# Four edits to a fused adapter/FFN/Sinkhorn kernel: low parts of the stacked operand formed once, root table loaded elsewhere, Sinkhorn shares 11, 12, 13, 13, base-weight blocks split sooner (and three smaller ones)

## The reference, cut to what matters

```python
# x: (8, 256, 1024); layer 0: a weight per sample, then a quantised FFN
h = einsum('bij,bkj->bik', x, weight[ids_cond])            # A: conditioned product
h = layernorm(h) * gamma + beta
h = fake_quant(h) @ fake_quant(w1).T + b1
x = x + (fake_quant(gelu(h)) @ fake_quant(w3).T + b3)
# layer 1: base linear + LoRA of rank 16, then stream mixing
base  = einsum('bsi,oi->bso', x, weight) + bias
y     = base + scale[id] * (x @ A[id].T @ B[id].T)
n     = y * rsqrt(mean(y*y) + eps)
H_res = sinkhorn(n @ W_res.T + base_res, 50 iterations)     # 4 x 4 per token
H_pre, H_post = softmax(n @ W_pre.T + ...), softmax(n @ W_post.T + ...)
H_res = (1 - g) * I + g * H_res
out   = x + H_res-mix(y) + (H_pre-gather(y) @ W_branch) spread by H_post
```

## Time and profile before

| | |
|---|---|
| median of 3 runs | 791.6 us (790.79 to 793.91) |
| profiled execution: its own time | 791.53 us |
| its span | 789.7 us |
| busy: TensorE, VectorE, ScalarE, GpSimd | 727.0, 555.2, 374.2, 68.0 us |
| mean granted TensorE clock | 0.971 of full |

### The profile page before, as it was taken

One profiled execution on the slowest core, in us unless ns is written; L12 is line 12 of the kernel. 1 busy time (PEld: TensorE's weight loads), 2 busy tenths in 40 slices (PEclk: granted clock), 3 DMA queues, 4 the chain that ended last, 5 costly groups with the idle time before them and its releaser, 6 DMA issues.

```text
span 789.7 us, 10179 instructions
## 1 busy us (share of the span) xinstructions
PE 727.0 (92%) x3228; PEld 490.2 (62%) x3228; DVE 555.2 (70%) x1933; ACT 374.2 (47%) x682; POOL 68.0 (9%) x40
## 2 busy tenths in 40 slices
PE   9989999999999999989998999998999994799937
PEld 6555444364656666434765788887878773567626
DVE  4558675537888887782865513517898988999985
ACT  2253735316556454543543643436324342699614
POOL 0002000200202022533031000000000000000000
PEclk9999999999999999999999999999999998799969
DMA  7959974243555542826032203113032157665406
GB/s 297 411 171 405 268 271 150 81 161 98 187 182 187 187 173 81 310 76 227 27 134 92 99 26 120 55 67 118 5 120 71 52 170 251 216 216 184 138 0 213
DMA packets 54279, 124.32 MB, mean 157 GB/s; under 512 B 8015, under 2 KB 33743, under 8 KB 48722
## 3 DMA queue, kind: packets, MB, share of 16 engines
q1 hardware_dynamic: 52930, 120.94, 44.1%
q10 hardware_dynamic: 1296, 2.74, 0.9%
HBM read 98.47 MB, written 25.19 MB: 157 GB/s over the span
## 4 chain that ended last, share of the span: by engine, by line
PE 52%; DVE 20%; ACT 10%; DMA 10%; issue 5%; SPq 2%; POOL 1%; ACTq 0%; DVEq 0%
PE PS L1080 15%; PE PS L969 10%; PE PS L905 8%; DMA stage<-w_dram 4%; PE PS L894 4%; DMA wscale_scratch<-wsc 3%; PE PS L958 2%; PE PS L1232 2%; PE PS L1192 2%; PE PS L1002 2%; DVE xp L1494 2%; DMA out_dram<-mr 2%; ACT blk L834 2%; DVE hbuf L1293 2%; PE PS L1186 2%
## 5 line engine op out<-in xcount | busy, mean ns | idle before, releaser
L905 PE MATMUL PS<-w_raw,x_raw 128*128 128x512 f32 x336 | 150.0, 600 | 4.7 <-DMA x_raw<-x_tr_dram 3.4
L905 PEld LDWEIGHTS PS<-w_raw,x_raw 128*128 128x128 f32 x336 | 63.1, 193 | 76.8 <-issue 73.2
L1080 PE MATMUL PS<-w_hi,xT_hi 128*128 128x512 f32 x256 | 103.3, 404 | 0.0
L1080 PE MATMUL PS<-w_hi,xT_lo 128*128 128x512 f32 x256 | 100.5, 393 | 0.0
L1080 PE MATMUL PS<-w_lo,xT_hi 128*128 128x512 f32 x256 | 100.3, 392 | 0.0
L514 POOL TENSOR_TENSOR xres<-xres,vecs 128x1024 f32<-128x1024 f32 x16 | 42.8, 2696 | 311.5 <-DMA xres<-x_tok_dram 311.5
L1399 DVE TENSOR_TENSOR xT_lo<-PS,xT_hi 128x512 fp32r<-128x512 f32 x32 | 20.6, 682 | 66.0 <-ACT xT_hi L662 65.8
L1588 DVE TENSOR_REDUCE ksum<-kprod 128x16 f32<-128x64 f32 x392 | 66.1, 209 | 0.0
L595 ACT ACTIVATE qT<-PS,round_c 128x512 bf16<-128x512 f32 x64 | 40.1, 678 | 45.7 <-PE PS L958 45.6
L969 PE MATMUL PS<-w3q,qT 128*128 128x512 bf16 x256 | 58.0, 379 | 1.0 <-ACT qT L595 1.0
L969 PE MATMUL PS<-w1q,qT 128*128 128x512 bf16 x256 | 57.9, 379 | 0.8 <-ACT qT L595 0.7
(11 more groups left out here) (190 smaller groups left out, 1393.8 us busy)
## 6 DMA issues: line engine op xcount, KB each, us to landing
w_raw<-cond_w_dram SPq DMA_DIRECT2D x31, 1024.0 KB, 5.7
x_raw<-x_tr_dram SPq DMA_DIRECT2D x32, 256.0 KB, 6.4
stage<-w_dram SPq DMA_DIRECT2D x16, 512.0 KB, 12.1
xres<-x_tok_dram SPq DMA_DIRECT2D x8, 1024.0 KB, 8.3
x_scratch<-x1buf SPq DMA_DIRECT2D x16, 512.0 KB, 5.1
x1n<-x_scratch SPq DMA_DIRECT2D x16, 512.0 KB, 6.1
y_scratch<-y SPq DMA_DIRECT2D x16, 512.0 KB, 3.1
stage<-base_w_nat_dram SPq DMA_DIRECT2D x8, 512.0 KB, 12.5
```

The source lines that it names most:

```text
L905: mm = pe.matmul(PS[:, 2 * t + h, :], x_raw[pr][:, c, t * P:(t + 1) * P], w_raw[pr][:, c, h * H2:(h + 1) * H2], start=(pr == 0 and c == 0) ...
L1080: pe.matmul(PS[:, 2 * t + h, :], xx[:, c, t * P:(t + 1) * P], ws[c // 2][:, c % 2, h * H2:(h + 1) * H2], start=(c == 0 and xx is xT_hi and ...
```

## The change

1. A DRAM table `low_dram` (129 rows) receives the low parts of all eight samples' rows and of the bias row. `load_rows` (SP) loads 8 x 16 rows and their scales after the stage loads of sample 1; ScalarE writes `all_hi` and `one_hi`, VectorE the differences, in place; `store_rows` stores them. Head columns follow at samples 4 to 6 (`store_heads`, `load_heads`, `store_head_rows`). In layer 1, rows 32 to 48 of `estage` are loaded from `low_dram`; the VectorE instruction of `lo_stacks` is gone, and `low_rank` waits for `e_hi`.
2. In `step_b` a Sqrt of a constant stands ahead of `evac_y(b, 1)`.
3. `B_ITERS` is (11, 12, 13, 13), with shares 2,3,3,3; 3,3,3,3; 3,3,3,4; 3,3,3,4, and none behind sample 7.
4. `split_hi(2)` stands in sample 6, `split_hi(3)` sooner in sample 7, `split_lo(2)` ahead of an `add_b3`. The heads' store and its wait leave the queue's place ahead of the loads `load_x1n`.
5. `keep_warm`: 48 transposes of the identity on TensorE, three iterations before the second Sinkhorn's end. The last tile's add and store are done in two halves.

```diff
@@ sync @@
+            def load_rows():
+                for b in range(NB):
+                    a = sp.value_load(ids[0:1, 1, bass.ds(b, 1)], min_val=0, max_val=NA - 1)
+                    r = slice(b * RANK, (b + 1) * RANK)
+                    sp.dma_start(all_in[r, :], lora_bt[bass.ds(a, 1), :, :].rearrange("a r n -> (a r) n")).then_inc(all_ld, 16)
+                    sp.dma_start(all_scale[r, :], scaling[bass.ds(a, 1), :].to_broadcast([RANK, 1])).then_inc(all_ld, 16)
...
             load_stage(KC + 7)
+            sp.wait_ge(st_T, 2 * (KC + 4))
+            sp.dma_start(one_in[:, :], bias_row).then_inc(all_ld, 16)
+            load_rows()
             load_xres(0)
             load_w(2, 0)
...
             for s in range(2, NB - 1):
+                if s == 2:
+                    store_rows()
+                if s == 4:
+                    store_heads()
+                if s == 5:
+                    load_heads()
+                if s == 6:
+                    store_head_rows()
...
-            sp.wait_ge(c_sb, 2)
-            sp.dma_start(c_dram.rearrange("a r n -> (a r) n"), csb[:, 0, :]).then_inc(c_st, 16)
-            sp.dma_start(cb_dram, csb[0:1, 1, :]).then_inc(c_st, 16)
-            sp.wait_ge(c_st, 32)
...
-                wait(sp, e_lo, b)
-                for r in (0, 32, 64):
+                wait(sp, e_hi, b)
+                sp.dma_start(estage[32:32 + RANK, :], low_dram[RANK * b:RANK * (b + 1), :]).then_inc(e_ld, 16)
+                for r in (0, 64):
@@ gpsimd @@
             split_lo(0)
             split_lo(1)
+            split_lo(2)
             add_b3(GUEST - 2)
-            split_lo(2)
             split_lo(3)
@@ scalar @@
             evac_stage(KC + 4)
+            act.wait_ge(all_ld, 16 * (2 * NB + 1))
+            nc.scalar.activation(all_hi[:, :], all_in[:, :], ACT.Copy, scale=all_scale[:, 0:1]).then_inc(all_high, 1)
+            nc.scalar.activation(one_hi[:, :], one_in[:, :], ACT.Copy).then_inc(all_high, 1)
             evac_T(0, 1, 1)
             gelu(0, 0)
...
                     evac_xT(b + 1, 0)
+                nc.scalar.activation(hd[:, 6, 0:1], round_c[:, 0:1], ACT.Sqrt)
                 evac_y(b, 1)
@@ tensor @@
             def low_rank(b, t, h):
                 pe.wait_ge(ls_done, b + 1)
-                pe.wait_ge(e_lo, b + 1)
+                pe.wait_ge(e_hi, b + 1)
...
+            def keep_warm():
+                pe.wait_ge(hs_step, 2)
+                pe.wait_ge(k_step[0], K0 + 3 + K_OPS * (SINKHORN - 1 - WARM_ITERS))
+                for i in range(WARM_LAST):
+                    pe.transpose(PS[:, SEL_BANK + i // 4 % 2, (i % 4) * P:(i % 4 + 1) * P], ident[:, :], ident[:, :])
...
+            keep_warm()
             select(1)
@@ vector @@
             quantise_stage(KC + 6)
             dve.wait_ge(bias_ld, 16 * 2)
             dve.wait_ge(swld, 16)
+            dve.wait_ge(all_high, 2)
+            nc.vector.scalar_tensor_tensor(out=all_in[:, :], in0=all_in[:, :], scalar=all_scale[:, 0:1],
+                                           in1=all_hi[:, :], op0=ALU.mult, op1=ALU.subtract).then_inc(all_low, 1)
+            nc.vector.tensor_tensor(one_in[:, :], one_in[:, :], one_hi[:, :], ALU.subtract).then_inc(all_low, 1)
             finish_w1(0, 0)
...
             def lo_stacks(b):
-                dve.wait_ge(e_hi, b + 1)
-                nc.vector.scalar_tensor_tensor(out=es[32:64, :], in0=estage[32:64, :], scalar=e_scale[32:64, 0:1],
-                                               in1=es[32:64, :], op0=ALU.mult, op1=ALU.subtract).then_inc(e_lo, 1)
                 dve.wait_ge(f_done, b + 1)
...
-                        n = B_ITERS // 4
-                        iterations(0, (b - NB // 2) * B_ITERS + i * n, n)
+                        k = b - NB // 2
+                        lo, hi = B_ITERS[k] * i // 4, B_ITERS[k] * (i + 1) // 4
+                        iterations(0, sum(B_ITERS[:k]) + lo, hi - lo)
```

More of the change, by code:

```diff
@@ L70, in adaln_ffn @@
         part_s.close()
+        part_e = ctx.enter_context(ExitStack())
+        for i in range(2 * PAIRS):
+            sb_in(part_e, f"below_rows{i}", [P, D], F32)
+        all_in = sb_in(part_e, "all_in", [NB * RANK, D], F32)
+        all_hi = sb_in(part_e, "all_hi", [NB * RANK, D], F32R)
+        one_in = sb_in(part_e, "one_in", [1, D], F32)
+        one_hi = sb_in(part_e, "one_hi", [1, D], F32R)
+        part_e.close()
+        part_n = ctx.enter_context(ExitStack())
+        heads_in = sb_in(part_n, "heads_in", [NB * RANK, NH], F32)
+        heads_hi = sb_in(part_n, "heads_hi", [NB * RANK, NH], F32R)
+        bias_in = sb_in(part_n, "bias_in", [1, NH], F32)
+        bias_hi = sb_in(part_n, "bias_hi", [1, NH], F32R)
+        part_n.close()
         part_w = ctx.enter_context(ExitStack())
@@ L206, in adaln_ffn @@
         vec_ld, bias_ld, ids_ld, ones_set = sem("vec_ld"), sem("bias_ld"), sem("ids_ld"), sem("ones_set")
-        high = [sem(f"high{i}") for i in range(PAIRS)]
-        low = [sem(f"low{i}") for i in range(PAIRS)]
+        high = [sem(f"high{i}") for i in range(PAIRS - 1)]
+        low = [sem(f"low{i}") for i in range(PAIRS - 1)]
         id_zero, id_set = sem("id_zero"), sem("id_set")
@@ L258, in adaln_ffn @@
         SK_OPS = 12
-        B_ITERS = 12
+        B_ITERS = (11, 12, 13, 13)
+        K0 = 3 + K_OPS * (SINKHORN - 1) + 1
+        WARM_ITERS, WARM_LAST = 3, 48
         @block.sync
@@ L311, in load_scales, with store_rows, load_heads, store_head_rows @@
                              ).then_inc(swld, 16)
+            def load_rows():
[4 more added lines that the diff above has]
+                    sp.dma_start(all_scale[r, :], scaling[bass.ds(a, 1), :].to_broadcast([RANK, 1])).then_inc(all_ld, 16)
+            def store_rows():
+                sp.wait_ge(all_low, 2)
+                sp.dma_start(low_dram[0:NB * RANK, 0:D], all_in[:, :]).then_inc(all_st, 16)
+                sp.dma_start(low_dram[NB * RANK:NB * RANK + 1, 0:D], one_in[:, :]).then_inc(all_st, 16)
+            def load_heads():
+                sp.wait_ge(c_st, 32)
+                sp.dma_start(bias_in[:, :], cb_dram).then_inc(all_ld, 16)
+                for b in range(NB):
+                    a = sp.value_load(ids[0:1, 1, bass.ds(b, 1)], min_val=0, max_val=NA - 1)
+                    sp.dma_start(heads_in[b * RANK:(b + 1) * RANK, :],
+                                 c_dram[bass.ds(a, 1), :, :].rearrange("a r n -> (a r) n")).then_inc(all_ld, 16)
+            def store_head_rows():
+                sp.wait_ge(all_low, 4)
+                sp.dma_start(low_dram[0:NB * RANK, D:D + NH], heads_in[:, :]).then_inc(all_st, 16)
+                sp.dma_start(low_dram[NB * RANK:NB * RANK + 1, D:D + NH], bias_in[:, :]).then_inc(all_st, 16)
             def load_xres(s):
@@ L489, in _ @@
                     load_mix(j + MIX)
-            for i in range(GROUP):
+            for i in range(GROUP - 1):
                 sp.wait_ge(f_add, i + 1)
                 sp.dma_start(streams(out[GROUP + i]), nr[i][:, :, :]).then_inc(n_st, 16)
+            for h in range(2):
+                sp.wait_ge(f_add, GROUP + h)
+                sp.dma_start(streams(out[NT - 1])[:, 2 * h:2 * h + 2, :], nr[GROUP - 1][:, 2 * h:2 * h + 2, :]).then_inc(n_st, 16)
             for i in range(MIX):
                 sp.wait_ge(o_st[i], GROUP // MIX * 16)
-            sp.wait_ge(n_st, 16 * GROUP)
+            sp.wait_ge(n_st, 16 * (GROUP + 1))
         @block.gpsimd
@@ L1664, in _ @@
             step_b(NB - 1, last=True, sink=True)
-            iterations(0, NB // 2 * B_ITERS, SINKHORN - 1 - NB // 2 * B_ITERS)
+            assert sum(B_ITERS) == SINKHORN - 1
             sinkhorn_finish(0)
@@ L1683, in last_add @@
             def last_add(i):
+                if i == GROUP - 1:
+                    for h in range(2):
+                        dve.wait_ge(fm_done, GROUP + h)
+                        nc.vector.tensor_tensor(nr[i][:, 2 * h:2 * h + 2, :].rearrange("p j c -> p (j c)"),
+                                                PS[:, 2 * (i % 2) + h, :],
+                                                nr[i][:, 2 * h:2 * h + 2, :].rearrange("p j c -> p (j c)"), ALU.add).then_inc(f_add, 1)
+                    return
                 dve.wait_ge(fm_done, i + 1)
```

42 lines of the change are left out of this document (32 added, 10 removed).

## The result

The changed kernel takes 780.27 us (median of 4 executions, 780.07 to 782.51) against 792.75 of the kernel before on the same chip (790.79 to 795.04): a ratio of 0.9848, 95% interval 0.9813 to 0.9883. The forecast was 776.7 in 771 to 784, faster with 0.92: the side and the range hold, the time is 3.6 us above it. The profiled execution spans 778.3 us, 11.4 less than the 789.7 before, where I had 14.8.

A forecast was written before the change was run, and what follows sets the result against it. TensorE was taken to bind up to sample 7 of layer 1, then VectorE. 4.5 + 0.2 - 6.4 - 9.5 - 1.3 - 1.5 - 0.8 = -14.8 on 789.7 gives 774.9, with 1.8 outside the span 776.7 us (771 to 782; range 771 to 784).

The forecast's parts named there:

- What bounds the kernel: Whole kernel: TensorE, busy 92% of the span, binds up to sample 7 of layer 1; behind it VectorE's second Sinkhorn.
- Early rows: Start of layer 0: small loads and new rows delay VectorE and then TensorE, a loss of 4.5 us (2.4 to 6.2).
- GpSimd holds VectorE: Rival, early rows: VectorE waits for GpSimd's whole bias add and TensorE's clock falls; 6.2 for 4.5, 778.4 us; chance 0.12.
- Heads' table: Beside samples 4 to 6: nine loads, two stores, four activations and differences cost 0.2 us (0 to 0.6).
- The guest: Layer 0, sample 7: earlier splits remove TensorE's weight wait and half clock, 5.2 less 0.5; with x1n's 1.7, 6.4 us gained.
- Layer 1: Table load and per-sample difference leave the path to xp and ls; 9.5 us gained (8.5 to 10.7).
- what stays in sample 4: Layer 1, sample 4: ls then hangs on ScalarE, coming from the exponentials; 0.3 us of the gain is not had.
- 0.8 stays: Layer 1, sample 7: a fourth Sinkhorn iteration in sample 6's last share leaves 0.8 of the 1.76 us unsaved.
- Table load behind sample 7: Sample 7's own table load, ahead of its softmax, no longer delays VectorE's second Sinkhorn; 1.3 us gained.
- The end: Behind the second Sinkhorn: 1.5 us gained by keep_warm and 0.8 by halving the last add and store, 2.3 in all.
- the warm-up misses: Rival, end: select is late by 1.7 and the clock falls in the pause; 3.2 us more, 780; 0.17 shared with another.
- A clock of 0.5 beside the last products: Sign of being wrong, at the end: a clock of 0.5 beside the eight last products.
- signs of being right: Layer 0's sample 7 weight and x1n waits gone; none at L1104; periods near 30.4; TensorE pause of 3 to 5 us.

## Why the prediction was right, and where it was off

**What bounds the kernel: right.** Up to sample 7 of layer 1 each stretch followed TensorE's waits, and behind it VectorE's end.

**Early rows, 4.5 forecast, 5.6 measured (5.8 to 6.5 in six further traces of kernels with the same rows).** The step that failed is the one on GpSimd: I said that the add lies beside `L1336` and stretches it by 2.0, and took off some since it "may miss the instruction". It hit, and not that instruction but the ones ahead of it, the quantisations and my own new difference, for 2.1 each (0.7 of the first is no news: in the kernel before the two quantisations took 2.15 for 1.41, beside the end of the same addition). TensorE's clock then fell behind the idle of 3.84, the other term of my 6.2. The rival *GpSimd holds VectorE* is what happened; it had 0.12. Without GpSimd the rows cost 2.1 to 2.4, the low end that I had worked out from their durations and the slack of 0.84. The row at one partition was not stretched (1.21), as it began 1.01 after GpSimd's end; by the page "SBUF — State Buffer" of the Trainium skill, section "Who interferes with whom", an instruction of VectorE that reads two inputs from SBUF and one of GpSimd that reads SBUF exclude each other, and the later of them is blocked until the other ends. The trace agrees to 0.2 us: the difference ends 1.08 behind GpSimd's 84.16, where it takes 1.28 alone.

**Heads' table, 0.2: right,** nothing of it is seen; the stretch with x1n is 1.75 shorter against 1.7.

**The guest, 4.7 forecast, 3.5 measured.** Both gains are there whole: no wait for weights, no half clock, 5.2. The size that was off is the 0.5 for three GpSimd instructions back to back; it is 1.42 + 0.24 = 1.7, within the 0 to 2 that I gave.

**Layer 1, 9.5 forecast, 10.7 measured.** The mechanism was right and the floor was wrong: I took 30.77 - 0.43 = 30.34 for TensorE alone. It is 29.94, as a wait costs its length and some 0.4 of overlap. That is why the load's return cost 5.4 us for waits that grew from 0.5 to 3.0 (xp) and from 3.2 to 3.7 (ls). Over the five periods of the sum and sample 2 that is 2.4 us more gained than I had. Against it stands the other mis-sized term, what stays in sample 4: I put it at 0.3 us, and behind the wait of 0.88 for `ls` that period is 31.57 us, 1.6 above the floor. And some 2.3 of the 10.7 us (an estimate, above) are half clock behind two waits in the kernel before's trace; the changed kernel's trace has none in this stretch. The change of the shares was in the sum only as "0.8 stays" in sample 7. Measured against 12, 12, 12, 13 it is 1.4 lost, with a wait of 0.80.

**Table load behind sample 7, 1.3 forecast, 0.9 measured** (1.1 by the run with the load back).

**The end, 2.3 forecast, 0.8 measured.** `keep_warm` was to bring 1.5 and brought nothing in the first trace. The step that failed: 1.9 gained on `last`. Its size was off too: 64 products of 256 columns are, by the row of 7.03, 14.06 us and not the 13.8 that I took, so at most 1.6 was to be had (14.08 where the clock stayed up). The transposes did warm the clock for `select(1)`, whose 1.0 was spent by starting 1.06 late, and the pause of 2.36 then lost the rest. I had named that ("may lose that again") and had priced the rival *the warm-up misses* at 780, which is where the time came out, though in part by the early rows. A clock of 0.5 beside the last products was one of my signs of being wrong, and for this term it was. From the last group's end to the span's end it is 4.6 us for 5.5 before, which fits the 0.8 forecast for the halves of the last tile; no run undid them alone.

Start to 78.88 is 0.6 longer, ahead of VectorE's new rows, and varies by 1.9 over the traces (78.3 to 80.2). Sum: 0.6 + 1.1 - 0.2 + 1.2 - 0.1 - 1.2 + 0.4 + 1.5 = 3.3 of the 3.4 us between forecast and trace. What stays open is why the clock falls in some executions behind the short products at 169 and not in others; no run here was made to tell. Of my signs of being right, two are not whole: one wait for xp (0.55, in sample 1) is left, and by the marker of the prediction the periods of samples 4 and 7 are 31.57 and 31.32, where I allowed 31 for sample 7.

## What to carry to other kernels

A new instruction on VectorE should be looked at together with what GpSimd runs at that moment: the early rows lost more to that neighbour (3.5 us) than to their own length (2.1 to 2.4), the guest lost 1.4 to it, and one semaphore wait on GpSimd gave 3.5 us back. A wait of TensorE costs more than its length (0.84 for 0.44 here, and 4.0 for 1.84 where the clock fell behind it), so a floor is to be read from a period without waits, not from one with the wait subtracted. Warming up an engine is worth something only if the warm stretch reaches the work: 34 transposes ahead of the selection and 16 in the pause behind it did what 48 ahead of it did in one trace of eight. And an edit of 1 us is judged by the stretch that it touches, since the time of a whole execution moves by more for reasons of its own.
